# Graph network: nine groups of edges instead of fifteen take their table rows through selection matmuls

## The chip, the cores and the metric

The kernel runs on one core of a Trainium2 chip. The time is device microseconds of one execution of the whole kernel. Engines are called PE (TensorE; PEld is its weight load), DVE (VectorE), ACT (ScalarE), POOL (GpSimd) and SP (SyncE, which issues most DMAs).

## The reference, cut to what matters

There are 3125 nodes with 128 features each and 53125 edges, sorted by destination. Three SAGE layers run on the normalised nodes first, with their result added to `x`; then one GINE layer:

```
h = relu(layernorm(x))
messages = gelu((h[src] + edge_attr) @ We1 + be1) @ We2 + be2      # 53125 x 128
aggregated = segment_sum(messages, dst)                            # 3125 x 128
x = x + gelu(((1 + eps) * h + aggregated) @ Wu1 + bu1) @ Wu2 + bu2
```

The change touches the GINE layer alone, and there only the fetch of the row of each edge's source, `h[src] @ We1 + be1`.

## The kernel before

The program has two parts. The first (lines up to 612) builds the adjacency counts and runs the three SAGE layers as dense products on PE. At its end the 3125 rows of `h @ We1 + be1` are written to a table in HBM, and kept on chip too, as two parts of 25 blocks of 125 rows (`chosen`).

The second part, the edge stage, walks over 105 groups of edges, up to 4 tiles of 128 edges each. One loop over groups is written out for every engine, and every engine works its list in order, held by semaphores. A group gets its table rows in one of two ways.

By rows: POOL issues one indirect DMA per tile (L640), four for a group, into one of six row buffers (`RW`); before a group it waits until DVE has used the buffer of six groups ago. PE multiplies the edge features with We1 (`mix`, L1356, two groups ahead), DVE adds the gathered rows (L1016), ACT applies Gelu (L1171), and PE sums the messages by destination (`aggregate`, L1413), with one-hot windows that DVE makes (L886).

By selection, for the groups listed in `picked`: SP loads the sources' numbers, DVE compares them with the node numbers of each of the 25 blocks (L908, eight buffers), and PE multiplies each comparison with both parts of that block of `chosen` (`take_sources`, L1370, 50 matmuls for a group) on top of the edge features' product (L1352). The result has features on partitions, so ACT applies Gelu (L1161), PE turns it (`flip`, L1378), and ACT copies it (L1168). `selections(g)` spreads the 25 blocks of the next picked group evenly over the by-rows groups ahead of it. These groups need nothing of POOL.

With 15 shares the picked groups are 3, 9, 16, 23, 29, 36, 43, 50, 56, 63, 70, 76, 83, 90 and 97, so six or seven groups lie between neighbours, and about five blocks fall to each group. When all edge groups of a chunk of 500 nodes are summed, the chunk goes through the last two matrices (L1390 to L1402, L924) and is stored; there are seven chunks, and the last one ends the kernel.

Of the kernel before, what the change touches and what calls it, by code (L numbers as in the profile page):

```python
# [29 lines left out]
class Shapes:  # L30


    def __init__(self, n_nodes, n_edges):
        self.N, self.E = n_nodes, n_edges
        self.NP = 125
        self.NB = n_nodes // self.NP
        self.EP = 125
        self.TG = 5
        self.NG = n_edges // (self.EP * self.TG)
        self.NT = self.NG * self.TG  # L40
        assert self.NP * self.NB == n_nodes and self.NT * self.EP == n_edges and self.NG % 2 == 1
        self.CH = -(-n_nodes // BANK)
        self.NBC = 4
        self.NC = -(-self.NB // self.NBC)
        self.MARGIN = 30
        self.node_end = [min(n_nodes, (c + 1) * self.NBC * self.NP) for c in range(self.NC)]

        def last(per):
            groups = -(-n_edges // per)
            return [groups - 1 if e == n_nodes else  # L50
                    min(groups - 1, -(-(e + self.MARGIN) * n_edges // (n_nodes * per)) - 1) for e in self.node_end]
        self.FT = -(-n_edges // P)
        self.FTG = 4
        self.FG = -(-(self.FT - 1) // self.FTG) + 1
        self.SLOPE = P * self.FTG * n_nodes / n_edges
        self.LAST = (self.FT - 1) * P * n_nodes / n_edges
        self.window = [(max(0, int(min(g * self.SLOPE, self.LAST)) - self.MARGIN - 1),
                        min(n_nodes, int((g + 1) * self.SLOPE) + self.MARGIN + 3)) for g in range(self.FG)]
        self.W = max(hi - lo for lo, hi in self.window)
        self.SHARES = 15  # L60
        reach = self.FG - 2 * self.FTG
        self.picked = [self.FTG - 1 + i * (reach - self.FTG + 1) // (self.SHARES - 1) for i in range(self.SHARES)]
        self.node_group = [max(g for g in range(self.FG) if self.window[g][0] < e) for e in self.node_end]

        self.DT = 2
        self.build_group = last(self.EP * self.DT)
        self.DG = self.NT // self.DT
        self.GB = self.DG + 1
        self.DW = 20
        self.NX = 27  # L70
        self.A_COLS = 12 * self.NB
        self.B_FROM = 5 * self.NB
        assert self.NT % self.DT == 1 and self.DW * self.NB <= BANK
# [1952 lines left out]
```

## Time and profile before

| what | value |
|---|---|
| time, median of 3 runs | 923.64 us (922.36 to 934.27) |
| span of the profiled execution | 1042.6 us |
| PE busy | 890.9 us (85%) |
| POOL busy | 416.5 us (40%) |
| DVE busy | 573.3 us (55%) |
| indirect DMAs | 356 |

No time of the profiled execution is kept beside its span. The span is 119 us longer than the median of the timed runs, so a reader has to ask of every idle stretch whether the timed runs have it too. Busy time of PE has modelled ends, and matmuls overlap: the distance between starts of the same kind of row tells more.

### The profile page before, as it was taken

The page shows a single profiled execution, that of the slowest core. Times are in us where ns is not written, and L with a number is a line of the kernel's source. Part 1 is how long each engine was busy: PE and PEld are TensorE (multiplying, and loading weights), DVE is VectorE, ACT ScalarE, POOL GpSimd, SP SyncE. Part 2 cuts the span into 40 slices and gives each one's busy share as a digit, 9 for nine tenths or more (in the row PEclk, how much of TensorE's full clock was granted, in tenths as well). Part 3 has the DMA queues.
Part 4 walks back from the last instruction along what each step waited for, and adds up shares of the span by engine and source line. Part 5 has one row for each costly group of instructions (what it writes and reads, how often), then busy time and mean ns, then how long its engine had stood idle before and what let it go on. Part 6 is the DMA issues. An engine that isn't in the chain of part 4 may idle for free.

```text
span 1042.6 us, 14743 instructions
## 1 busy us (share of the span) xinstructions
PE 890.9 (85%) x4894; PEld 678.2 (65%) x4894; DVE 573.3 (55%) x1806; ACT 326.0 (31%) x575; POOL 416.5 (40%) x451
## 2 busy tenths in 40 slices
PE   4978999999999999767958987797899859788966
PEld 2834555557778777655747776575777647667865
DVE  8399999983544455446633364453545425444521
ACT  3376677762555544401101111110111110111111
POOL 1000000000222222276866666567566654675640
PEclk9969999999999999976968998898798879888986
DMA  4200000010000000183322332333333322333310
GB/s 128 59 2 11 12 3 12 13 21 1 1 1 1 11 13 17 47 210 95 112 79 78 112 116 74 88 114 109 107 95 109 101 83 81 94 97 94 117 56 15
DMA packets 37389, 67.51 MB, mean 65 GB/s; under 512 B 14625, under 2 KB 24828, under 8 KB 37180
## 3 DMA queue, kind: packets, MB, share of 16 engines
q1 hardware_dynamic: 25916, 43.15, 13.8%
q0 software_dynamic: 11392, 23.35, 8.5%
q8 instruction: 41, 0.67, 0.3%
q14 instruction: 40, 0.33, 0.1%
HBM read 63.18 MB, written 3.30 MB: 64 GB/s over the span
## 4 chain that ended last, share of the span: by engine, by line
PE 74%; issue 9%; DVE 8%; another core or an unknown queue 6%; ACT 1%; DMA 1%; ACTq 0%; SPq 0%; DVEq 0%
PE f_ps L1370 18%; PE f_ps L1315 13%; PE f_ps L1413 10%; PE f_ps L1356 8%; PE f_ps L1308 8%; PE f_ps L1192 3%; PE f_ps L1185 2%; PE f_ps L1282 2%; PE f_ps L1244 1%; DVE f_select L908 1%; DVE f_region L692 1%; DVE f_region L690 1%; PE f_ps L1203 1%; PE f_ps L1352 1%
## 5 line engine op out<-in xcount | busy, mean ns | idle before, releaser
L640 POOL DMA_INDIRECT f_adj<-table,f_by_edge x356 | 364.6, 1024 | 205.6 <-issue 102.5
L1370 PE MATMUL f_ps<-f_select,f_pair 125*128 125x512 f32 x750 | 228.1, 447 | 38.0 <-issue 23.6
L908 DVE TENSOR_SCALAR f_select<-f_offset 128x512 fp32r<-128x512 f16 x375 | 147.0, 439 | 180.8 <-PE f_ps L1370 111.2
L1370 PEld LDWEIGHTS f_ps<-f_select,f_pair 125*128 125x128 f32 x750 | 150.0, 209 | 94.9 <-issue 45.0
L625 POOL CAST f_wide<-f_adj 125x500 fp32r<-125x500 uint8 (+1 forms) x70 | 40.6, 580 | 372.4 <-ACT f_adj L1048 226.6
L1413 PE MATMUL f_ps<-f_adj 128*128 128x94 f32 (+20 forms) x984 | 141.9, 287 | 31.3 <-issue 31.1
L1413 PEld LDWEIGHTS f_ps<-f_adj 128*128 128x128 f32 x984 | 140.8, 210 | 37.4 <-issue 30.6
L1315 PE MATMUL f_ps<-f_wide,f_pair 125*128 125x500 f32 (+1 forms) x700 | 162.6, 385 | 1.6 <-DVE f_wide L749 0.6
L1171 ACT ACTIVATE f_adj<-f_adj 128x512 f32<-128x512 f32 (+1 forms) x90 | 56.2, 625 | 336.4 <-DVE f_adj L1016 272.7
L1048 ACT CAST f_adj<-f_ps 128x500 f32 x213 | 126.1, 592 | 62.4 <-PE f_ps L1192 47.4
L1315 PEld LDWEIGHTS f_ps<-f_wide,f_pair 125*128 125x128 f32 x700 | 122.2, 189 | 33.6 <-issue 6.2
L1356 PE MATMUL f_ps<-f_We,f_region 128*128 128x128 f32 x712 | 116.5, 305 | 25.5 <-issue 17.8
L1308 PE MATMUL f_ps<-f_adj,f_parts 125*128 125x500 fp8e4 (+1 forms) x525 | 127.9, 352 | 0.0
L1356 PEld LDWEIGHTS f_ps<-f_We,f_region 128*128 128x128 f32 x712 | 101.2, 214 | 31.6 <-issue 26.0
L886 DVE SCALAR_TENSOR_TENSOR f_adj<-f_iota,f_dst_abs 128x376 f32<-128x376 f16 (+4 forms) x105 | 56.0, 535 | 94.1 <-remote 70.4
L1102 ACT CAST f_wide<-f_adj 125x500 fp32r<-125x500 uint8 (+1 forms) x140 | 78.1, 565 | 60.6 <-PE f_ps L1315 59.7
L1185 PE MATMUL f_ps<-f_region 125*128 125x300 f16 (+1 forms) x213 | 66.4, 312 | 24.2 <-DVE f_region L696 23.3
L749 DVE CAST f_wide<-f_adj 125x500 fp32r<-125x500 uint8 (+1 forms) x140 | 57.7, 422 | 52.9 <-PE f_ps L1315 52.6
L690 DVE TENSOR_SCALAR f_region<-f_iota,f_by_edge 125x300 f16<-125x300 f16 x212 | 62.6, 295 | 22.7 <-PE f_ps L1192 22.3
L1192 PE MATMUL f_ps<-f_region 125*128 125x375 f16 x212 | 73.0, 344 | 0.0
L692 DVE TENSOR_SCALAR f_region<-f_iota,f_by_edge 125x375 f16<-125x375 f16 x212 | 67.5, 318 | 0.0
L1308 PEld LDWEIGHTS f_ps<-f_adj,f_parts 125*128 125x128 bf16 x525 | 47.4, 97 | 25.1 <-issue 1.7
(146 smaller groups left out, 717.0 us busy)
## 6 DMA issues: line engine op xcount, KB each, us to landing
f_region<-in_edge_attr_T SPq DMA_DIRECT2D x34, 768.0 KB
f_adj<-table,f_by_edge POOLq DMA_INDIRECT x356
f_src_rows<-in_src_row SPq DMA_DIRECT2D x15, 256.0 KB
f_adj<-inv SPq DMA_DIRECT2D x1, 1562.5 KB
table<-f_region SPq DMA_DIRECT2D x6, 250.0 KB
out<-f_xT SPq DMA_DIRECT2D x6, 250.0 KB
f_rcntT<-inv SPq DMA_DIRECT2D x5, 250.0 KB, 3.7
f_xT<-in_xT SPq DMA_DIRECT2D x1, 812.5 KB, 6.3
```

What stands on the lines that cost most here:

```text
L640: pool.indirect_dma_start(out=rows[:, r % RW, j * D:(j + 1) * D], out_offset=None, in_=table, in_offset=bass.IndirectOffsetOnAxis(ap=table ...
L692: dve.tensor_scalar(keys[0:EP, slot, s.A_COLS:KEYS], iota[0:EP, s.B_FROM:s.DW * NB], key[0:EP, tt + 1:tt + 2], None, ALU.is_equal)
L908: dve.tensor_scalar(select[:, u % SELECT, :], offset[:, i % 2, :], float(b * NP - CENTRE), None, ALU.is_equal).then_inc(select_ready, 1)
L1048: act.copy(adj[:, :, bass.ds(base, s.DW)], ps[:, build_ps(g):build_ps(g) + s.DW * NB].rearrange("p (w b) -> p b w", b=NB)).then_inc(kept, 1)
L1102: act.copy(wide_tile(u), bytes_of(u)).then_inc(widened[ON_ACT], 1)
L1185: pe.matmul(ps[:, o:o + wide], lows[0:EP, slot, 0, :], keys[0:EP, slot, 0:wide], start=True, stop=g == 0, skip_group_check=True)
L1192: ins = pe.matmul(ps[:, o + s.B_FROM:o + s.DW * NB], lows[0:EP, slot, 1, :], keys[0:EP, slot, s.A_COLS:KEYS], start=False, stop=True, skip ...
L1308: ins = pe.matmul(ps[:, dense_ps(i):dense_ps(i) + width(c)], parts1[0:NP, p, b, :], adj[0:NP, b, lo:hi].bitcast(F8), start=b == 0 and p == ...
L1315: ins = pe.matmul(ps[:, dense_ps(i):dense_ps(i) + streamed(c)], pair[l][0:NP, p, b, :], wide_tile(u), start=b == 0 and p == 0, stop=b == N ...
L1356: ins = pe.matmul(z_ps(g, j), edge_tiles(g, j, j + 1), weights["We1"][:, :], start=True, stop=True)
L1370: ins = pe.matmul(z_columns(g), chosen[0:NP, p, b, :], select[0:NP, u % SELECT, :], start=b == 0 and p == 0, stop=b == NB - 1 and p == 1, ...
L1413: ins = pe.matmul(agg_ps(c, lo, hi), msg[:, g % MS, j * D:(j + 1) * D], onehot[:, g % OH, j, at_lo:at_lo + hi - lo], start=opens and j == ...
```

## The change

`SHARES` falls from 15 to 9. The picked groups become 3, 14, 26, 38, 50, 61, 73, 85 and 97: six fewer, farther apart, each with its 25 blocks spread over some ten groups instead of five. The other 96 groups go by rows. Nothing else is changed; the first and the last picked group stay where they were.

```diff
-        self.SHARES = 15
+        self.SHARES = 9
         reach = self.FG - 2 * self.FTG
         self.picked = [self.FTG - 1 + i * (reach - self.FTG + 1) // (self.SHARES - 1) for i in range(self.SHARES)]
```

## Rows read from the trace of the kernel before

**Rows 1.** Busy time by stretch: before, during and after the indirect DMAs.

```profile
core 0: us, PE busy (x) PEld busy (x) DVE busy (x) ACT busy (x) POOL busy (x), PEclk, DMA share, GB/s
0.00:442.40 442.40, 410.71 (x2293) 278.88 (x2293) 301.58 (x1176) 246.81 (x441) 51.92 (x95) 0.98 0.08 20
442.40:1010.70 568.30, 458.47 (x2498) 380.95 (x2498) 265.10 (x616) 74.25 (x124) 364.56 (x356) 0.85 0.35 102
1010.70:1042.60 31.90, 21.68 (x103) 18.39 (x103) 6.61 (x14) 4.91 (x10) 0.00 (x0) 0.70 0.04 15
```

**Rows 2.** Chain that ended last, by line, from 442.4 on; its longest wait.

```profile
by line: PE f_ps L1370 31.9%; PE f_ps L1413 17.0%; PE f_ps L1356 14.6%; issue 14.4%; another core or an unknown queue 10.3%; DVE f_select L908 1.8%; PE f_ps L1352 1.5%; PE f_ps L1390 1.2%; PE f_ps L1378 1.1%; DVE f_adj L1016 0.8%; PE f_ps L
...
837.96 18.44 another core or an unknown queue
```

**Rows 3.** Timeline, 850 to 870: start, duration, engine, line [idle before, releaser].

```profile
852.44 0.94 POOL L640 DMA_INDIRECT f_adj<-table,f_by_edge  x1 [0.30 <-issue]
856.42 0.55 DVE L886 SCALAR_TENSOR_TENSOR f_adj<-f_iota,f_dst_abs 128x376 f32<-128x376 f16 x1 [13.82 <-remote]
...
857.55 1.11 PE L1378 MATMUL f_ps<-f_ident,f_flipping 128*128 128x128 f32 x4 [12.27 <-ACT f_flipping L1161]
...
866.24 0.95 POOL L640 DMA_INDIRECT f_adj<-table,f_by_edge  x1 [12.86 <-DVE f_adj L1016]
```

**Rows 4.** Line L640: durations in ns, and what ended POOL's idle time.

```profile
L640 POOL DMA_INDIRECT f_adj<-table,f_by_edge x356: 941/947/3013, 442.5 to 1009.7; - x178
...
  issue: 102.5, 331
  DVE f_adj L1016: 101.2, 24
```

**Rows 5.** Groups of instructions by line: count, busy us, mean ns, idle before.

```profile
L640 POOL DMA_INDIRECT f_adj<-table,f_by_edge x356 | 364.6, 1024 | 205.6 <-issue 102.5 <-DVE f_adj L1016 101.2 <-DMA table<-f_region 1.9
L1370 PE MATMUL f_ps<-f_select,f_pair 125*128 125x512 f32 x750 | 228.1, 447 | 38.0 <-issue 23.6 <-DVE f_select L908 13.6
...
L908 DVE TENSOR_SCALAR f_select<-f_offset 128x512 fp32r<-128x512 f16 x375 | 147.0, 439 | 180.8 <-PE f_ps L1370 111.2 <-remote 53.2 <-issue 15.2
L1413 PE MATMUL f_ps<-f_adj 128*128 128x94 f32 (+20 forms) x984 | 141.9, 287 | 31.3 <-issue 31.1
...
L1356 PE MATMUL f_ps<-f_We,f_region 128*128 128x128 f32 x712 | 116.5, 305 | 25.5 <-issue 17.8 <-DMA f_region<-in_edge_attr_T 5.4 <-DVE f_select L908 1.1
```

**Rows 6.** Timeline, 976 to 983: by-rows groups with five blocks each.

```profile
977.59 1.08 PE L1356 MATMUL f_ps<-f_We,f_region 128*128 128x128 f32 x8
...
978.32 1.81 DVE L908 TENSOR_SCALAR f_select<-f_offset 128x512 fp32r<-128x512 f16 x5
...
978.46 1.09 POOL L640 DMA_INDIRECT f_adj<-table,f_by_edge  x1 [0.30 <-issue]
...
981.67 1.08 PE L1356 MATMUL f_ps<-f_We,f_region 128*128 128x128 f32 x8
```

**Rows 7.** Timeline, 1003.8 to 1010: groups without blocks.

```profile
1003.92 0.60 PE L1378 MATMUL f_ps<-f_ident,f_flipping 128*128 128x128 f32 x4
...
1006.15 1.03 PE L1413 MATMUL f_ps<-f_adj 128*128 128x94 f32 x8
...
1007.93 1.03 PE L1413 MATMUL f_ps<-f_adj 128*128 128x94 f32 x8
```

**Rows 8.** Busy time in two stretches of the edge stage, and an aggregate in the second.

```profile
976.00:988.00 12.00, 12.00 (x78) 10.82 (x77) 8.85 (x22) 2.17 (x4) 9.26 (x10) 1.00 0.54 187
1013.50:1024.00 10.50, 10.36 (x49) 10.34 (x49) 3.25 (x8) 2.09 (x4) 0.00 (x0) 0.50 0.01 2
```
```profile
1015.53 3.48 PE L1413 MATMUL f_ps<-f_adj 128*128 128x50 f32 x16
```

**Rows 9.** Timeline of the end: the last indirect DMA and the last instruction on DVE.

```profile
1009.74 0.95 POOL L640 DMA_INDIRECT f_adj<-table,f_by_edge  x1 [0.30 <-issue]
...
1034.81 0.35 DVE L924 SCALAR_TENSOR_TENSOR f_xT<-f_ps,f_bu,f_xT 128x125 f32<-128x125 f32 x1 [1.52 <-PE f_ps L1402]
```

## The prediction

> **What bounds the kernel now.** I read the stretches first, cut at the first and the last indirect DMA. Up to 442.4 us PE works at a granted clock of 0.98 and POOL hardly at all; the edge stage takes 568.3 us at a clock of 0.85, and 31.9 us follow it [rows 1]. The change touches the last two alone, so 442.5 us are fixed.
>
> Next I read the chain that ended last. From 442.4 us on it runs through PE, through its selections (L1370, 31.9%) above all, and this would make PE the bound. But 14.4% of that chain is "issue" and 10.3% an unknown queue, together 148 us of 600 [rows 2]. The longest such wait shows what they are: PE stands still for 12.27 us, DVE has waited 13.82, and they start again within 1.2 us of each other with nothing recorded that released them, while POOL goes on issuing until its six buffers are full and is then 12.86 us late [rows 3]. The profiled execution is 119 us longer than the median, and these waits are the only place of that size that I can find for it. So I take most of them to belong to that execution, and the chain there isn't the chain of the timed runs.
>
> So I work out the edge stage without them, engine by engine.
>
> POOL: 947 ns is the median of an indirect DMA, and 102.5 us over 331 gaps make 0.310 us between two of them where POOL waits for nobody (0.30 in most) [rows 4]. That gives a bare 1.25 us for each DMA, 5.0 us for a group, and 356 x 1.25 = 445 us. With the mean of 1024 ns [rows 5] it is 364.6 + 102.5 = 467 us.
>
> PE at full clock: a group with five blocks takes 981.67 - 977.59 = 4.08 us [rows 6], one without blocks 1007.93 - 1006.15 = 1.78 us [rows 7], so a block costs (4.08 - 1.78) / 5 = 0.46 us. 105 x 1.78 + 375 x 0.46 + 15 flips x 0.60 = 187 + 172 + 9 = 368 us. Of 984 aggregate matmuls [rows 5], 832 (416 tiles, two each) are in the 1.78; the other 152, where a group straddles two chunks, take 152 x 1.78 / 16 = 17 us. That is 385 us, and the node chunks come on top. From above, PE is busy for 458 + 22 = 480 us at the clocks of the profile [rows 1]. An estimate of 410 us at full clock lies nearer the lower end, since a mean clock of 0.85 means that 0.3 of that time ran at half clock.
>
> The end: from the last DMA to the last DVE instruction lie 25.4 us, and 7.4 more to the end of the span [rows 9]. In it PE worked at a clock of 0.50 [rows 8]. At full clock the 25.4 would halve; so the end takes 20 to 33 us.
>
> If POOL is the bound, the kernel takes between 442.5 + 445 + 20 = 908 us and 442.5 + 467 + 33 = 943 us. The median, 923.64, lies in the middle. Turned round, it leaves 448 to 461 us for 356 DMAs, or 1.26 to 1.30 us for each: between the bare 1.25 and the 1.31 of the trace, with room for 3 to 16 us at most in which POOL waits or is slowed. I read from this that in the timed runs POOL issues nearly without a break, and PE, with some 410 us, follows.
>
> **The change part by part.**
>
> Added, on POOL: six groups x 4 tiles = 24 indirect DMAs. At 1.25 us [rows 4] they cost 30.0 us, at 1.30 us 31.1. All of it lies on POOL's own list, where nothing hides it. Who waits for it: DVE's addition (L1016) waits for the rows, and behind that, on DVE, stand the comparisons for the next group, so PE's selections are held too; each waits at POOL's pace, as before.
>
> Removed, on PE: 150 blocks x 0.46 = 69 us and six flips x 0.60 = 4 us [rows 6, 7], 73 us together. The features' product stays in another shape (one or the other 0.9 us). At the stage's mean clock of 0.85 it would be 85 us. If POOL is the bound, this is worth nothing on the path; its cover is POOL's 475 us against PE's remaining 337.
>
> Removed, on DVE: 150 comparisons of 439 ns [rows 5], with six additions of rows in return. DVE is busy 265 of 568 us [rows 1], so for itself this is nothing. ACT gives up a Gelu and a copy for each of the six groups and gets one Gelu; it is busy 74 us [rows 1]: nothing. SP loads six lists of sources fewer while the gathers bring 24 tiles more; the DMA engines have a share of 0.35 [rows 1]: nothing.
>
> Indirect, from DVE to POOL: an indirect DMA beside a comparison takes 1.09 us in place of 0.947 [rows 6, 4]. All excess over the median in the trace is 356 x 77 ns = 27 us [rows 4, 5]. The comparisons fall by 40%, so at most 27 x 0.4 = 11 us come back; with the 3 to 16 us that the timed runs leave, 1 to 6 us, and nothing excludes that all 16 go. I take 4 us. For this the Trainium skill (SBUF — State Buffer, section Who interferes with whom) has a rule: a comparison of this kind can hold a port that DVE and GpSimd share, and the other is then blocked for its whole duration. By it each of the 150 comparisons might give back its 0.42 us, 63 us in all, and the time would be near 891 us; the trace shows 0.14 us for one hit and not all are hits, so it is borne out as to who disturbs whom and not in that size.
>
> The end: PE has less behind it when the last rows land. Between 0 and 5 us; I take 2, nearer to nothing, as there are no blocks after group 95 in either kernel.
>
> Sum, made on the median, since the profiled span has 119 us that I don't carry over: 923.64 + 30 - 4 - 2 = 948 us. With the ends of the unknown terms, 923.64 + 30 - 16 - 5 = 933 to 923.64 + 31 = 955.
>
> The profiled span of the changed kernel can go either way: the waits that lie on PE's list there may become fewer with fewer instructions.
>
> **The rivals.**
>
> PE is the bound, as the chain says, and the change is faster. For it: 410 us at the stage's granted clock of 0.85 are 482, and 442.5 + 482 is the median too, about. Then POOL would have to be cheaper in the timed runs than in the trace. The point from which it decides: with 26 us for the end, 380 DMAs end at the median for (923.64 - 442.5 - 26) / 380 = 1.20 us each; below 1.15 us the kernel is over 2% faster. If the 0.30 us between two DMAs belonged to the profiled execution, a DMA would take 0.947, POOL 360 us, and PE would set the time: 923.64 - 73 = 851 us. Against it: the gap has 0.30 us in PE's busiest stretch and in the one where PE stands still alike [rows 6, 3]. Price 851 to 905; chance 0.11.
>
> No change that can be told from none (2% here, 905 to 942 us). POOL is the bound, but much of the 24 DMAs is paid by what it no longer loses: all 16 us that the median leaves, with a quicker end, or with 27 us of excess all gone: 923.64 + 30 - 27 = 927. Or a DMA takes 1.20 us. The rows cap the first by 40% fewer comparisons. Price 922 to 939; chance 0.10.
>
> PE's clock falls and PE becomes the bound after all. With 337 us of work in 475, PE pauses in every group. In the profile PE is granted 0.50 after a wait and does 16 aggregate matmuls in 3.48 us, where at a clock of 1.00 they take 1.78 [rows 7, 8]. PE would need a mean clock under 337 / 475 = 0.71 to be the slower one; at 0.66 it takes 511 us, and the kernel 442.5 + 511 + 12 = 965. Against it: once PE falls behind, it has no pauses, and in the profile it comes back to 1.00 [rows 8]. The Trainium skill (TensorE: Matmul & The Clock Gate, section HAM oscillation) says as much: pauses between bursts of matmuls can throttle PE again and again. Chance 0.05.
>
> **How the numbers follow.** The forecast, POOL sets the pace and 24 DMAs come on top, has 0.74; 0.06 of that lies below 942 us. Slower by over 2%: 0.68 + 0.05 = 0.73. Within 2%: 0.10 + 0.06 = 0.16. Faster: 0.11. The range leaves out the faster rival and the clock's fall, 0.16 together, and takes in the rest: 922 to 958 us.
>
> **What the profile of the changed kernel would show.** Right: 380 indirect DMAs, still 1.25 us from start to start where nobody waits, fewer of them at 1.09 us or more; 450 selections on PE in place of 750; much less than 101 us of POOL waiting for DVE's L1016 [rows 4]; more of ACT's and DVE's waits ended by landed rows, and PE idle between groups. The first would fail if POOL's DMAs stand closer than 1.20 us. Wrong would be a time under 922 us: then the 0.30 us gap isn't in the timed runs, or PE's waits, which I gave to the profiled execution, are in them as well.

## The result, and the profile after

The changed kernel takes 947.15 us (median of 4 runs, 946.93 to 947.99) against 923.36 us before (median of 4, 922.36 to 934.27). It is slower, by 23.8 us; the forecast was 948 us. The ratio over all of these runs is 1.0235, with a 95% interval of 1.020 to 1.027; the medians alone stand as 1.026 to 1, since the 934.27 hardly moves a median.

The stretches of the kernel after, cut at its first and last indirect DMA as in [rows 1]:

```profile
core 0: us, PE busy (x) PEld busy (x) DVE busy (x) ACT busy (x) POOL busy (x), PEclk, DMA share, GB/s
0.00:434.60 434.60, 402.33 (x2293) 272.31 (x2293) 301.58 (x1176) 246.28 (x441) 51.75 (x95) 0.98 0.09 20
434.60:926.60 492.00, 395.41 (x2292) 347.54 (x2292) 214.28 (x474) 74.36 (x123) 376.34 (x380) 0.86 0.40 118
926.60:945.00 18.40, 7.93 (x21) 4.92 (x21) 2.81 (x6) 2.03 (x5) 0.00 (x0) 0.53 0.08 25
```

The edge stage takes 492.0 us, and PE is busy in only 395 of them, where [rows 1] had 458 of 568. Its granted clock is 0.86. What bounds the stage is seen in the chain that ended last, by line, from 435 us on (the answer to [rows 2]):

```profile
by line: POOL f_adj L640 64.8%; issue 24.1%; PE f_ps L1413 1.2%; PE f_ps L1370 0.9%; PE f_ps L1356 0.8%; DVE f_adj L1016 0.8%; PE f_ps L1398 0.5%; PE f_ps L1402 0.5%; DMA f_adj<-table,f_by_edge 0.5%; DVE f_select L908 0.3%; DVE f_adj L886 0
```

"issue" is here mostly POOL's own time between two DMAs. PE's lines together are under 5%, where PE's selections alone had 31.9% in [rows 2]. The line of the indirect DMAs (durations in ns: least, median, longest; then what ended the idle time before them), beside [rows 4], and the groups beside [rows 5]:

```profile
L640 POOL DMA_INDIRECT f_adj<-table,f_by_edge x380: 940/944/2667, 434.7 to 925.6; - x190
...
  issue: 114.6, 376
...
  DVE f_adj L1016: 0.9, 3
```
```profile
L640 POOL DMA_INDIRECT f_adj<-table,f_by_edge x380 | 376.3, 990 | 117.4 <-issue 114.6 <-DMA table<-f_region 1.9 <-DVE f_adj L1016 0.9
L1370 PE MATMUL f_ps<-f_select,f_pair 125*128 125x512 f32 x450 | 142.9, 456 | 3.5 <-DVE f_select L908 3.5
L1356 PE MATMUL f_ps<-f_We,f_region 128*128 128x128 f32 x760 | 126.2, 319 | 73.1 <-DVE f_adj L1016 60.5 <-DMA f_region<-in_edge_attr_T 12.1
...
L908 DVE TENSOR_SCALAR f_select<-f_offset 128x512 fp32r<-128x512 f16 x225 | 86.9, 437 | 0.4
```

380 DMAs, 114.6 / 376 = 0.305 us between two of them, and 0.9 us of waiting for DVE in the whole stage. PE now waits 60.5 us for DVE's additions (L1016). The profile puts only 8.6 us of the additions' own waits down to a landing DMA and leaves most of the rest without a releaser, but their starts tell: 66 of the 96 start less than 2.2 us after the last DMA of their group has ended on POOL, 56 of them 1.5 to 1.8 us after it. So most of them wait for rows. A stretch of the timeline shows how the rows arrive. Three DMAs are lengthened, the first beside a window build (L886), the other two beside comparisons (L908), and DVE's addition starts late with a landing DMA named as what held it.

```profile
690.61 0.55 DVE L886 SCALAR_TENSOR_TENSOR f_adj<-f_iota,f_dst_abs 128x376 f32<-128x376 f16 x1 [1.10 <-PE f_ps L1413]
690.81 1.16 POOL L640 DMA_INDIRECT f_adj<-table,f_by_edge  x1 [0.30 <-issue]
...
692.19 0.69 DVE L1016 TENSOR_TENSOR f_adj<-f_ps,f_adj 128x512 f32<-128x512 f32 x1 [1.03 <-DMA f_adj<-table,f_by_edge]
692.28 1.05 POOL L640 DMA_INDIRECT f_adj<-table,f_by_edge  x1 [0.31 <-issue]
692.80 1.09 DVE L908 TENSOR_SCALAR f_select<-f_offset 128x512 fp32r<-128x512 f16 x3
...
693.64 1.07 POOL L640 DMA_INDIRECT f_adj<-table,f_by_edge  x1 [0.30 <-issue]
...
695.01 0.94 POOL L640 DMA_INDIRECT f_adj<-table,f_by_edge  x1 [0.30 <-issue]
...
696.26 0.94 POOL L640 DMA_INDIRECT f_adj<-table,f_by_edge  x1 [0.30 <-issue]
```

### The profile page after: what moved, and what is told of

Read it like the earlier page. It is cut to its first block, busy times and chain, and to the rows that moved or that the text cites. A ratio compares the mean times of both kernels' runs of the same rounds, so it can differ in the third digit from the quotient of the medians.

```text
span 945.0 us, 14011 instructions
## 1 busy us (share of the span) xinstructions
PE 805.7 (85%) x4606; PEld 624.8 (66%) x4606; DVE 518.7 (55%) x1656; ACT 322.7 (34%) x569; POOL 428.1 (45%) x475
## 4 chain that ended last, share of the span: by engine, by line
PE 39%; POOL 36%; issue 14%; DVE 8%; ACT 1%; DMA 1%; ACTq 0%; POOLq 0%; SPq 0%; DVEq 0%
POOL f_adj L640 36%; PE f_ps L1315 15%; PE f_ps L1308 9%; PE f_ps L1192 3%; PE f_ps L1185 3%; PE f_ps L1282 2%; PE f_ps L1244 1%; DVE f_region L692 1%; DVE f_region L690 1%; DVE f_region L696 1%; DVE f_region L694 1%; PE f_ps L1203 1%; PE f_ps L1413 1%; PE f_ps L1293 1%; PE f_ps L1206 1%
## 5 line engine op out<-in xcount | busy, mean ns | idle before, releaser
L640 POOL DMA_INDIRECT f_adj<-table,f_by_edge x380 | 376.3, 990 | 117.4 <-issue 114.6
L1016 DVE TENSOR_TENSOR f_adj<-f_ps,f_adj 128x512 f32<-128x512 f32 (+1 forms) x96 | 65.8, 685 | 263.7 <-issue 207.5
L1171 ACT ACTIVATE f_adj<-f_adj 128x512 f32<-128x512 f32 (+1 forms) x96 | 60.1, 626 | 387.7 <-DVE f_adj L1016 377.1
L1356 PE MATMUL f_ps<-f_We,f_region 128*128 128x128 f32 x760 | 126.2, 319 | 73.1 <-DVE f_adj L1016 60.5
L1356 PEld LDWEIGHTS f_ps<-f_We,f_region 128*128 128x128 f32 x760 | 111.9, 226 | 78.0 <-issue 65.0
L1413 PEld LDWEIGHTS f_ps<-f_adj 128*128 128x128 f32 x984 | 146.9, 221 | 17.4 <-DVE f_adj L886 5.8
L1413 PE MATMUL f_ps<-f_adj 128*128 128x94 f32 (+20 forms) x984 | 144.1, 298 | 5.2 <-ACT f_adj L1171 5.0
L1370 PE MATMUL f_ps<-f_select,f_pair 125*128 125x512 f32 x450 | 142.9, 456 | 3.5 <-DVE f_select L908 3.5
L1370 PEld LDWEIGHTS f_ps<-f_select,f_pair 125*128 125x128 f32 x450 | 89.7, 212 | 27.4 <-DVE f_select L908 7.6
L908 DVE TENSOR_SCALAR f_select<-f_offset 128x512 fp32r<-128x512 f16 x225 | 86.9, 437 | 0.4
```

The lines of the kernel that those rows point to most:

```text
L640: pool.indirect_dma_start(out=rows[:, r % RW, j * D:(j + 1) * D], out_offset=None, in_=table, in_offset=bass.IndirectOffsetOnAxis(ap=table ...
L908: dve.tensor_scalar(select[:, u % SELECT, :], offset[:, i % 2, :], float(b * NP - CENTRE), None, ALU.is_equal).then_inc(select_ready, 1)
L1356: ins = pe.matmul(z_ps(g, j), edge_tiles(g, j, j + 1), weights["We1"][:, :], start=True, stop=True)
L1370: ins = pe.matmul(z_columns(g), chosen[0:NP, p, b, :], select[0:NP, u % SELECT, :], start=b == 0 and p == 0, stop=b == NB - 1 and p == 1, ...
L1413: ins = pe.matmul(agg_ps(c, lo, hi), msg[:, g % MS, j * D:(j + 1) * D], onehot[:, g % OH, j, at_lo:at_lo + hi - lo], start=opens and j == ...
```

## The experiments

The theory is the prediction's: POOL, with one indirect DMA after another, sets the time of the edge stage, and comparisons on DVE slow it a little. The rivals: PE is the bound; or something else in the change counts, such as the order of the groups or PE's clock. The kernel before was run beside each, with medians of 925.3 to 925.5 us in these sessions; ratios are against it, over all runs, and so not quite those of the medians. The kernel after was not run beside them, so a difference to its 947.15 us carries the 2 us by which the kernel before differs from its 923.36.

**The kernel before, profiled once more (no edit).**

> The kernel before, unchanged, for a second profile of it. Theory (POOL sets the pace): 923 us, POOL's 356 indirect DMAs stand 1.25 to 1.30 us apart from the first to the last, it waits under 16 us in all for DVE's additions, and the chain runs through POOL. Rival (PE is the bound): the chain runs through PE's selections, and POOL waits tens of us for buffers.

Its execution takes 925.34 us, with a span of 923.5. So this profile, unlike the first, is one of an execution as long as the timed runs. Its stretches, the chain from 435 us on, and the DMAs by line and by group:

```profile
0.00:431.70 431.70, 400.54 (x2293) 271.07 (x2293) 301.61 (x1176) 246.23 (x441) 51.78 (x95) 0.98 0.09 20
431.70:904.80 473.10, 432.83 (x2580) 377.11 (x2580) 269.36 (x624) 77.30 (x129) 364.74 (x356) 0.92 0.43 123
904.80:923.50 18.70, 7.93 (x21) 4.91 (x21) 2.81 (x6) 2.03 (x5) 0.00 (x0) 0.51 0.08 24
```
```profile
by line: POOL f_adj L640 53.4%; issue 17.2%; PE f_ps L1370 5.5%; DMA inv<-f_rstd 3.4%; PE f_ps L1413 2.8%; DMA f_region<-in_edge_attr_T 2.8%; PE f_ps L1356 2.7%; PE f_ps L1398 0.8%; PE f_ps L1402 0.7%; DMA f_adj<-table,f_by_edge 0.6%; DVE f
```
```profile
L640 POOL DMA_INDIRECT f_adj<-table,f_by_edge x356: 940/947/2632, 431.8 to 903.8; - x178
...
  issue: 107.3, 352
...
  DVE f_adj L1016: 0.9, 3
```
```profile
L640 POOL DMA_INDIRECT f_adj<-table,f_by_edge x356 | 364.7, 1025 | 109.8 <-issue 107.3 <-DMA table<-f_region 1.6 <-DVE f_adj L1016 0.9
```

The chain runs through POOL here too, with PE's lines on it for about an eighth; the unknown queue is gone from it, and POOL waits 0.9 us for DVE where [rows 4] had 101.2. Only the distance of the DMAs misses what was expected: (903.8 - 431.8) / 355 = 1.33 us and not 1.25 to 1.30. The waits that the prediction gave to the first profiled execution did belong to it. The 0.30 us between two DMAs did not: the gap is the same in this one.

**Half of the selection matmuls left out of the kernel before.**

```diff
-                for p in range(2):
+                for p in range(1):
...
-                                    start=b == 0 and p == 0, stop=b == NB - 1 and p == 1, skip_group_check=True)
+                                    start=b == 0 and p == 0, stop=b == NB - 1 and p == 0, skip_group_check=True)
```

> The kernel before, with the second part of each block's matmuls left out (375 of 750 selection matmuls, so the low part of the selected rows is missing from the sums); DVE and POOL have the same lists. PE is relieved of 375 x 0.23 = 86 us at full clock. Theory: 923 us less 0 to 10, since POOL still issues 356 DMAs. Rival (PE is the bound): up to 86 us faster, 840 to 880 us.

926.39 us, a ratio of 1.0015 (0.9986 to 1.0044). PE's busy time in the stage falls to 384 us (from 432.83), and the time stays. POOL takes as long as before:

```profile
L640 POOL DMA_INDIRECT f_adj<-table,f_by_edge x356: 940/945/3692, 432.3 to 906.0; - x178
```

This rules out the first rival: with fifteen groups, PE's selections don't set the time, though the chain above names them for 5.5%.

**24 DMAs left out of the kernel after.**

```diff
+        self.no_rows = [20, 32, 44, 56, 67, 79]
...
                 r = s.by_rows(g)
+                if g in s.no_rows:
+                    continue
                 for j in range(s.tiles(g)):
...
```

The part left out changes DVE's wait for landed rows, which no longer counts the DMAs of these groups.

> The kernel after, with the indirect DMAs of six of its by-rows groups left out (20, 32, 44, 56, 67 and 79: DVE adds what the row buffer held before, so the messages of these edges are of other sources). POOL is back at 356 DMAs; PE, DVE and ACT keep the lists of the kernel after. Theory (POOL sets the pace): 947 - 24 x 1.29 = 916 us, and so some 7 us under the kernel before, since 150 comparisons fewer disturb POOL. Rival (the order of the groups, spread wider, or PE's clock made it slow): it stays near 947 us.

915.36 us, a ratio of 0.9886 (0.982 to 0.995) to the kernel before, 31.8 us under the kernel after. PE, DVE and ACT have the lists of the kernel after, in its order, so neither the order nor the clock made it slow; the DMAs did. The forecast of 916 is met, and its second half too, with 9.9 us for some 7: with 356 DMAs in both, this kernel is faster than the one before. POOL's stretch says where from:

```profile
L643 POOL DMA_INDIRECT f_adj<-table,f_by_edge x356: 940/944/2642, 432.2 to 894.2; - x178
```

894.2 - 432.2 = 462.0 us against 903.8 - 431.8 = 472.0.

**150 comparisons added on DVE in the kernel after; comparisons made narrow in the kernel before.** The first adds two comparisons that nobody reads in each of 75 groups, on two scratch buffers by turns. The second keeps all comparisons, on 64 columns in place of 512.

```diff
...
+                        if 4 <= r < 79:
+                            for i in range(2 * (r - 4), 2 * (r - 4) + 2):
+                                if i >= 2:
+                                    dve.wait_ge(extra, i - 1)
+                                dve.tensor_scalar(work[:, i % 2, :].bitcast(F32R), iota[:, :], 3.0, None, ALU.is_equal
+                                                  ).then_inc(extra, 1)
```
```diff
-                dve.tensor_scalar(select[:, u % SELECT, :], offset[:, i % 2, :], float(b * NP - CENTRE), None,
+                w = T * P if u < SELECT else 64
+                dve.tensor_scalar(select[:, u % SELECT, 0:w], offset[:, i % 2, 0:w], float(b * NP - CENTRE), None,
                                   ALU.is_equal).then_inc(select_ready, 1)
```

> The kernel after, with 150 comparisons of 500 columns added on DVE that nobody reads (two in each of 75 by-rows groups), so DVE compares as often as in the kernel before. Theory (comparisons on DVE slow POOL's DMAs): the mean indirect DMA goes back from 990 ns towards 1025, 380 x 0.035 = 13 us, so 954 to 962 us. By the rule that a comparison blocks GpSimd for its whole duration: up to 150 x 0.42 = 63 us, 1010 us. Rival (no such effect; the DMAs of the kernel before are slower for another reason): 947 us.

> The kernel before, with all comparisons after the first eight on 64 columns in place of 512 (so most selections are stale and the selected rows are not those of the sources). As many instructions everywhere, but each comparison on DVE is short. Theory (comparisons slow POOL): the mean indirect DMA falls from 1025 ns to 960 to 990, and the time by 12 to 23 us, to 900 to 912. Rival (no such effect): 925 us.

952.62 us with more of them (ratio 1.0271, 1.0207 to 1.0336), 5.5 us over the kernel after and under the 954 to 962 that were expected; 908.70 us with narrow ones (0.9811, 0.9751 to 0.9871). The DMAs of the two, and the narrow comparisons:

```profile
L641 POOL DMA_INDIRECT f_adj<-table,f_by_edge x380: 940/945/3306, 432.2 to 931.8; - x190
```
```profile
L641 POOL DMA_INDIRECT f_adj<-table,f_by_edge x380 | 385.1, 1013 | 117.2 <-issue 115.5 <-DMA table<-f_region 1.7
```
```profile
L640 POOL DMA_INDIRECT f_adj<-table,f_by_edge x356: 940/944/2818, 431.9 to 887.7; - x178
```
```profile
L640 POOL DMA_INDIRECT f_adj<-table,f_by_edge x356 | 348.6, 979 | 109.9 <-issue 108.2 <-DMA table<-f_region 1.7
...
L909 DVE TENSOR_SCALAR f_select<-f_offset 128x64 fp32r<-128x64 f16 (+1 forms) x375 | 61.6, 231 | 67.7 <-PE f_ps L1371 66.3
```

The median DMA takes 944 to 947 ns in these two kernels and in those before and after; the mean moves with DVE's comparisons, 990 to 1013 ns and 1025 to 979. POOL's stretch grows by 499.6 - 490.9 = 8.7 us, and shrinks by 472.0 - 455.8 = 16.2 us, nearly the whole change of the time (16.6 us). That comparisons slow POOL is shown by the narrow ones, in the time and in POOL's stretch. The added ones agree in the stretch, from one profile of each kernel; in the time they don't decide, since the interval of their ratio takes in that of the kernel after. By the rule of the Trainium skill (SBUF — State Buffer, section Who interferes with whom), such an operation can block GpSimd for its whole duration. Taken as a price for each comparison, that doesn't give the size: 150 comparisons of 0.45 us cost 8.7 us of POOL's time, 0.06 us each.

Comparisons aren't all of it. With each DMA laid beside what DVE does meanwhile, those that overlap neither a comparison nor a window build (L886) take 945 to 948 ns on average in all eleven profiles, additions beside them or not. In the second profile of before, the 165 that overlap a comparison average 1070 ns, and the 71 that overlap a window build and no comparison 1047. So window builds, 105 in every kernel, go with longer DMAs too. About half of what the added comparisons cost stands beside window builds and no comparison (8.4 us over 944 ns for each DMA, 3.6 in the kernel after); how that comes about is open.

**Other numbers of picked groups.** The same line of code with 12, 17, 18 and 20.

> Twelve picked groups in place of fifteen, 368 indirect DMAs in place of 356. Theory: 12 DMAs x 1.29 us = +15 us less some 2 us of contention, so 935 to 939 us, half way between the two kernels. Rival (PE is the bound in one of the two kernels and POOL in the other): the time bends, and lies under the middle, near 923 us or below it.

> Seventeen picked groups, 348 indirect DMAs. Theory (POOL sets the pace up to about eighteen): 912.65 + 4 x 1.29 = 918 us, with POOL not waiting for buffers. Rival (PE has been the bound since sixteen or seventeen): 900 to 910 us, since PE has 11 us less to do than with eighteen.

> Eighteen picked groups, 344 indirect DMAs, and three groups more of selections on PE. Theory: POOL alone would need 12 x 1.29 = 15 us less than in the kernel before (908 us), while PE needs some 15 us more at full clock on about 410, so that PE is no longer covered: 905 to 925 us, with POOL waiting for buffers. Rival (PE is the bound already with fifteen): 923 + 15 x (1 to 1.18) = 938 to 941 us.

> Twenty picked groups, 336 indirect DMAs. With eighteen the chain ran through PE in most of the edge stage, while POOL hardly waited. Theory: PE needs 2 x 11 = 22 us more than with eighteen, and is not covered any more, so 915 to 935 us, slower than with eighteen (912.65), with POOL waiting for buffers. Rival (POOL still sets the pace): 912 - 8 x 1.29 = 902 us.

| picked groups | indirect DMAs | time, us | ratio to before | POOL first to last DMA, us |
|---|---|---|---|---|
| 9 (after) | 380 | 947.15 | 1.0235 (1.020 to 1.027) | 490.9 |
| 12 | 368 | 931.96 | 1.0091 (1.0057 to 1.0125) | 478.3 |
| 15 (before) | 356 | 923.4 to 925.5 | 1 | 472.0 |
| 17 | 348 | 916.12 | 0.9886 (0.9855 to 0.9918) | 460.9 |
| 18 | 344 | 912.65 | 0.9860 (0.9826 to 0.9895) | 456.3 |
| 20 | 336 | 924.16 | 1.0005 (0.9968 to 1.0042) | 467.3 |

Twelve came out 3 us under what was expected: its DMAs have a mean of 998 ns, close to the 990 of nine groups and not half way to 1025. The excess over the median does not go in proportion with the comparisons (28 us with 375 of them, 20 with 300, 17 with 225); the window builds, as many in every kernel, are a part of why, and the rest is open. Up to 18 groups the time falls with POOL's stretch, though 17 and 18 can't be told apart by their intervals; with 20 it rises again, as expected. The groups of the DMAs with 18 and with 20, the chain with 18, and the edge stage with 20:

```profile
L640 POOL DMA_INDIRECT f_adj<-table,f_by_edge x344 | 352.7, 1025 | 106.5 <-issue 103.0 <-DMA table<-f_region 1.9 <-DVE f_adj L1016 1.5
```
```profile
L640 POOL DMA_INDIRECT f_adj<-table,f_by_edge x336 | 349.1, 1039 | 120.8 <-issue 98.9 <-DVE f_adj L1016 20.3 <-DMA table<-f_region 1.6
```
```profile
by line: PE f_ps L1370 35.0%; PE f_ps L1413 17.0%; PE f_ps L1356 12.6%; POOL f_adj L640 6.2%; DMA inv<-f_rstd 3.0%; DMA f_region<-in_edge_attr_T 2.8%; PE f_ps L1352 2.8%; issue 2.3%; PE f_ps L1398 1.3%; PE f_ps L1402 1.3%; PE f_ps L1378 1.2
```
```profile
431.60:900.00 468.40, 454.42 (x2755) 393.79 (x2756) 330.87 (x747) 77.83 (x131) 349.07 (x336) 0.98 0.41 124
```

POOL's waiting for DVE is 1.5 us with 18 and 20.3 with 20, where PE is busy in 454 of 468 us at a clock of 0.98: PE has become the bound. The turn is gradual. With 18 the chain is PE's already, and PE is busy in 443 of 456 us at a clock of 0.97, yet POOL still issues nearly without a break; the wait for buffers that was expected there did not come, and both engines are full. DVE's additions show the same turn: with nine groups 66 of 96 start less than 2.2 us after their group's last DMA, with 15 (second profile) 48 of 90, with 17 34 of 88, with 18 10 of 87, and with 20 none of 85. 18 groups beat both kernels, by 1.4% and 3.6%. 19 groups have no time: with them the engines' lists stop, each waiting for another. More than 20 were not run.

## Why the prediction was right

Step by step, with the two profiles of executions as long as the timed runs (the second of before, and that of after):

| term | predicted, us | measured, us |
|---|---|---|
| 24 indirect DMAs more | +30.0 | 24 x (0.944 + 0.305) = +30.0 |
| POOL less disturbed by DVE | -4 (0 to -16) | (490.9 - 472.0) - 30.0 = -11.1 |
| the end | -2 (0 to -5) | (945.0 - 925.6) - (923.5 - 903.8) = -0.3 |
| up to the first DMA | 0 | 434.7 - 431.8 = +2.9 |
| sum | +24 | +21.5; timed medians +23.8 |

The bound was right, and against the chain of the first profile. Reading [rows 2, 3] as waits of that execution alone was the step on which all hung; the second profile of before shows it, and the kernel with half of the selection matmuls shows that PE's 73 us less were worth nothing, as the prediction said. The price of a DMA from [rows 4] held to 0.01 us.

The relief of POOL was the term that was mis-sized, with 4 us taken and 9 to 11 measured: 11.1 in the table, 9.9 in the time and 10.0 in POOL's stretch when the 24 DMAs were left out, and 8.7 in the stretch when the comparisons were put back. It went wrong where the median was turned round: the room for POOL to be slowed was worked out with the first DMA at 442.5 us [rows 1], and in the second profile of before it stands at 431.8. With that, (923.5 - 431.8 - 19.7) / 356 = 1.33 us for each DMA, the mean of 1.025 and the gap of 0.305, and not 1.26 to 1.30. The 11 us that the prediction worked out from the trace itself, 27 x 0.4, was the right size.

The end did not get shorter: PE is busy for 8 us of it in both profiles, so it was not behind with fifteen groups either. The 2.9 us ahead of the first DMA don't belong to the change: that part has 2293 matmuls in both kernels, and the kernel before has had 442.5 and 431.8 us for it. That the forecast came out to 1 us is thus luck in part: the relief was 7 us larger than taken, and against it stood 1.7 us of the end, the 2.9 us, and 2.3 us by which the timed medians lie farther apart than the two profiled spans.

Of the rivals, a cheaper DMA in the timed runs fell with the unchanged 0.305 us gap. PE's clock did fall, from 0.92 to 0.86 in the edge stage, but PE was busy 395 of 492 us and POOL did not wait for it: POOL's waiting for DVE, behind which PE would stand, is 0.9 us in both. By the Trainium skill (TensorE: Matmul & The Clock Gate, section HAM oscillation), pauses between bursts of matmuls can throttle PE again; the fall of the clock agrees with it, and here it costs nothing.

Of the signs, 380 DMAs, 450 selections and an idle PE came. POOL's short wait for L1016 says nothing of the change, since the second profile of before has the same 0.9 us.

Three readings of rows were off, and the sum does not hang on them. In [rows 3] PE's wait does have a releaser, ACT's Gelu (L1161); those without one are DVE's wait and one of ACT's, 17.88 us, just ahead of that Gelu. The 1.78 us of [rows 7] are a group with eight aggregate matmuls and eight of the features' product, not 16 aggregates. And [rows 8] has the clock at 1.00 first and at 0.50 after it, so it shows no return to 1.00.

## What to carry to other kernels

When a profiled execution is much longer than the timed runs, work out each engine's sum without the waits that have no releaser, set it against the timed median, and don't trust the chain alone. Here two sums fitted, POOL's and that of PE at the stage's clock, so a second profile, of an execution as long as the timed runs, is worth more than either. Where two engines share work and a number sets the split, the time follows the engine with the longer sum until the other overtakes it, so both sums, not busy shares, tell which way to move the number. An engine that sets the time also gains from what its neighbours no longer do, and that term is worth sizing from its mean and its median duration. Why one indirect DMA takes 0.944 us and the next starts 0.305 us later, no run here shows.

## What the runs showed that was not expected

The part ahead of the first indirect DMA, which is the same in all these kernels, took 431.7 to 432.3 us in seven of the eleven profiles, 434.4 and 434.7 in two, and 442.5 and 442.7 in two others. The difference arises early: between 20 and 40 us, PE does this many matmuls in the second profile of before (first DMA at 431.8 us) and in that with 18 groups (442.7):

```profile
20.00:40.00 20.00, 20.00 (x152) 15.94 (x152) 12.58 (x61) 10.84 (x20) 0.00 (x0) 1.00 0.31 76
```
```profile
20.00:40.00 20.00, 20.00 (x77) 14.92 (x76) 7.30 (x37) 6.70 (x12) 0.00 (x0) 1.00 0.30 75
```

77 in place of 152, at the same clock. In the first profile of before (442.5) there are 78, and in that of after (434.7) 126, so it goes with the execution and not with the number of groups. It may bear on the spread of the times (921 to 937 us for the kernel before): the profiled execution with 18 groups took 921.22 us where their median is 912.65. What makes the difference was not looked into.
